# K of 14 head pairs in seven block products, and the exchange ahead of the q load, in a gated cross-attention kernel

## What is computed

```
x = _rmsnorm(hidden_states, ln_weight)
h_q = (x @ w_q.T).reshape(b, lq, H, DH)
h_k = (key_value_states @ w_k.T).reshape(b, lk, H, DH)
h_v = (key_value_states @ w_v.T).reshape(b, lk, H, DH)
score = jnp.einsum('bqhd,bkhd->bhqk', h_q, h_k) + position_bias[None]
score = softmax(where(m, score, -inf))
attn = jnp.einsum('bhqk,bkhd->bqhd', score, h_v).reshape(b, lq, H * DH)
return hidden_states + attn @ w_out.T
```

## Time and profile before

| | |
|---|---|
| median of 3 runs | 897.46 us |
| the profiled execution: its time | 903.37 us |
| its span, first to last instruction | 901.6 us |
| PE busy | 871.0 us (97%) |
| DVE, ACT, POOL busy | 54%, 40%, 33% |
| mean granted clock of PE | 0.998 |

### The profile page before, as it was taken

How to read it: one execution, slowest core, us unless ns; L and a number is a source line. 1 busy time by engine, 2 the same in 40 slices (tenths; PEclk the granted TensorE clock), 3 DMA queues, 4 the chain that set the end, 5 groups by cost and what they waited for, 6 DMA issues and landing times.

```text
span 901.6 us, 15022 instructions
## 1 busy us (share of the span) xinstructions
PE 871.0 (97%) x5128; PEld 769.5 (85%) x5128; DVE 486.7 (54%) x847; ACT 358.9 (40%) x966; POOL 301.2 (33%) x216
## 2 busy tenths in 40 slices
PE   8999999998999999999999999999999999999998
PEld 7878888887888988898989889898889898898786
DVE  6886565573627272636354362726263535577863
ACT  5654444553434342425253343434242525354320
POOL 1476665663232323314132323232231413332200
PEclk9999999999999999999999999999999999999999
DMA  9134545555243333424251524333342425151101
GB/s 312 39 105 158 179 151 175 174 176 198 67 150 99 116 116 99 154 85 146 69 183 37 187 65 151 110 105 122 108 148 76 154 61 190 35 201 34 38 24 70
DMA packets 50673, 109.69 MB, mean 122 GB/s; under 512 B 6752, under 2 KB 24160, under 8 KB 48736
## 3 DMA queue, kind: packets, MB, share of 16 engines
q1 hardware_dynamic: 50656, 109.47, 37.0%
HBM read 75.89 MB, written 33.55 MB: 121 GB/s over the span
## 4 chain that ended last, share of the span: by engine, by line
PE 64%; DMA 14%; DVE 12%; issue 4%; SPq 2%; ACT 1%; POOL 1%; DVEq 0%; POOLq 0%
PE proj_ps L1134 34%; PE proj_ps L1307 15%; DMA block_spill<-block_sb 9%; DMA attn<-block_spill 5%; DVE attn L912 3%; PE score_ps L1193 3%; PE proj_ps L1485 2%; PE turn_ps L1193 2%; PE pv_ps L1193 2%; DVE block_sb L932 2%; SPq L318 2%; DVE attn L926 2%; PE turn_ps L1165 1%; PE proj_ps L1503 1%; DMA acc<-in_x 1%
## 5 line engine op out<-in xcount | busy, mean ns | idle before, releaser
L372 POOL TENSOR_TENSOR w_lo<-w_raw,w_hi 128x1024 fp32r<-128x1024 f32 x49 | 117.1, 2391 | 312.9 <-ACT w_hi L466 312.8
L1134 PE MATMUL proj_ps<-w_hi,ct_hi 128*128 128x256 f32 x512 | 146.4, 286 | 0.0
L1134 PE MATMUL proj_ps<-w_hi,ct_lo 128*128 128x256 f32 x512 | 145.0, 283 | 0.0
L1134 PE MATMUL proj_ps<-w_lo,ct_hi 128*128 128x256 f32 x512 | 145.0, 283 | 0.0
L383 POOL TENSOR_TENSOR comb<-mask_add,bias_sb 128x1024 f32<-128x1024 f32 x32 | 76.7, 2417 | 131.4 <-DVE attn L926 127.6
L486 ACT ACTIVATE attn<-attn,neg_max 128x128 f32<-128x128 f32 x256 | 99.2, 389 | 52.6 <-DVE neg_max L915 52.6
L948 DVE TENSOR_TENSOR acc<-proj_ps,acc 128x512 f32<-128x512 f32 x112 | 77.5, 692 | 66.7 <-PE proj_ps L1134 65.8
L466 ACT ACTIVATE w_hi<-w_raw 128x1024 fp32r<-128x1024 f32 x49 | 51.8, 1059 | 121.9 <-PE proj_ps L1134 118.9
L1134 PEld LDWEIGHTS proj_ps<-w_hi,ct_hi 128*128 128x128 f32 x512 | 98.4, 192 | 0.7
L1134 PEld LDWEIGHTS proj_ps<-w_hi,ct_lo 128*128 128x128 f32 x512 | 98.3, 192 | 0.7
L1134 PEld LDWEIGHTS proj_ps<-w_lo,ct_hi 128*128 128x128 f32 x512 | 98.2, 192 | 0.0
(11 more groups left out here) (204 smaller groups left out, 1781.2 us busy)
## 6 DMA issues: line engine op xcount, KB each, us to landing
w_raw<-in_weights SPq DMA_DIRECT2D x67, 512.0 KB, 3.7
q_spill<-attn SPq DMA_DIRECT2D x60, 256.0 KB, 3.0
qt<-q_spill SPq DMA_DIRECT2D x15, 1024.0 KB, 7.9
block_spill<-block_sb SPq DMA_DIRECT2D x30, 512.0 KB, 4.0
attn<-block_spill SPq DMA_DIRECT2D x120, 128.0 KB, 2.9
acc<-in_x SPq DMA_DIRECT2D x4, 512.0 KB, 9.8
bias_sb<-in_bias SPq DMA_DIRECT2D x16, 128.0 KB, 2.9
out<-attn SPq DMA_DIRECT2D x8, 256.0 KB, 2.0
```

The source lines that it names most:

```text
L372: pool.tensor_tensor(lo, w_raw[:, k, :], hi.bitcast(F32), ALU.subtract).then_inc(w_lo_done[k], 1)
L1134: mm = pe.matmul(o, lhs(l, n), rhs(r, n), start=(start and n == 0 and m == 0), stop=(stop and n == terms - 1 and m == 2))
```

## The change

**K in seven products.** For pairs 2 to 15 (turns p = 2 to 15, index i = p - 2) k is made as q is: `k_stage(p)` makes seven products of 2 blocks x 3 = 6 matmuls, 42 of 512 columns. The products use five banks for results (`proj_ps1` twice, `proj_ps3` twice, `proj_ps2`, and the score banks `turn_ps` and `pv_ps`), so `pv_bank` gives the pv units the other order of banks (score_ps0, score_ps1, turn_ps, pv_ps). Turn 1 keeps the four chunks and is written out on each engine; the loops run from 2.

**Forms of the weights.** POOL makes four sums of 128x256 blocks (`ks_forms`, lines 490 to 495 of the changed file) and seven lo halves of 128x256 (line 500), ACT seven hi halves (line 742), a turn ahead, in place of one 128x1024 of each (`lead(WK)`, `rest(WK)`). ACT further takes three copies in place of four k copies, DVE four sums of products (`k_posts`), POOL one (`k_last_sum`, 128x512).

**Forms of the context.** T1 to T4 are made once, from float32 halves of the context that SP loads again (`load_block` 0 and 1 early in the q loop, 2 ahead of the last `q_phase`, 3 in turn 1): DVE subtracts, ACT leads (`lead_kt`), POOL rests (`rest_kt`), all 128x1024. Form 0 is made in the last `q_phase`, the others in turn 1.

**Order.** In a turn SP does the exchange first and the q load behind it; PE makes two v products ahead of `pv(a, 0)` in place of one. The weights of the last stage (`WQ` of NPH, `WK` of NPH) are split in the last turn; x is reloaded into `mask_add` for two of the eight tiles. In the last turn POOL waits for `probs_done` before `add_mask(LAST)` and adds `k_last_sum` behind it, and PE waits for it (`k_sum`) ahead of `scores(LAST, 0)`.

The diff, cut to its core:

```diff
@@ SP
+            load_block(0, k_buf[:, 0:2, :], 0, 0)
+            load_block(1, k_buf[:, 2:4, :], 0, 1)
...
+            sp.wait_ge(qa_lo, NQ * AF)
+            sp.wait_ge(s_step, NQ * SF)
+            load_block(2, w_raw[:, WQ, :].rearrange("p (c s) -> p c s", c=2), 1, 1)
...
-            with sp.Fori(1, LAST) as p:
-                load_q(p)
+            def turn(p):
                 for t in range(2):
                     exchange(p - 1, t)
+                if isinstance(p, int):
+                    sp.wait_ge(kt_done, 3)
+                    sp.wait_ge(kt_hi_done, 1)
+                    sp.wait_ge(kt_lo_done, 1)
+                    load_block(3, k_buf[:, 0:2, :], 1, 0)
+                load_q(p)
                 load_bias(p + 1)
-                refill(WK, p + 2)
+                sp.wait_ge(k_lo, p * PRODUCTS)
+                load_w(WK, p + 2)
                 refill(WV, p + 2)
                 refill(WO, p + 1)
@@ POOL
+            def k_last_sum(i):
+                pool.wait_ge(k_copied, i * COPIES + 2)
+                pool.wait_ge(k_post, i * KPOSTS + 2)
+                pool.tensor_tensor(kt[:, 1, half(1)], k_w, k_v, ALU.add).then_inc(k_sum, 1)
+
+            rest_kt(0, 1)
             pool.wait_ge(mask_done, 1)
             add_mask(0)
             rest(WK, 1)
             rest(WV, 1)
             rest(WO, 0)
...
+            with pool.Fori(2, LAST) as p:
                 pool.wait_ge(probs_done, (p - 1) * UNITS + UNITS)
                 add_mask(p)
-                for k in (WK, WV):
-                    rest(k, p + 1)
+                k_last_sum(p - 2)
+                k_forms(p - 1)
+                rest(WV, p + 1)
                 rest(WO, p)
@@ ACT, iteration(p)
                 exps(a, 0)
                 exps(a, 1)
+                k_copy(i, 1, s_copy, k1_ps)
                 exps(a, 2)
-                chunk(0)
+                k_copy(i, 2, k_w, k5_ps)
                 exps(a, 3)
-                chunk(1)
-                chunk(2)
-                chunk(3)
-                lead(WK, p + 1)
+                k_copy(i, 6, k_at(0), k1_ps)
                 lead_at(a, 0)
                 lead_at(a, 1)
...
+                v_copy(p, 1)
+                lead_k(i + 1)
                 lead_at(a, 2)
                 lead_at(a, 3)
@@ DVE, behind turn_probs(a, 1)
+            def k_posts(i):
...
+                post(4, k_t, k6_ps, s_copy)
+                post(5, k_v, k7_ps, k_t)
+                post(3, kt[:, 1, half(0)], k4_ps, k_v)
+                post(7, kt[:, 0, half(1)], k5_ps, k_t)
@@ PE
+            def k_product(o, w, x, start=True):
+                for c in range(2):
+                    for m, (l, r) in enumerate(((0, 0), (1, 0), (0, 1))):
+                        mm = pe.matmul(o[:, :], w[l][:, c, :], x[r][:, c, :], start=(start and c == 0 and m == 0),
+                                       stop=(c == 1 and m == 2), skip_group_check=not start)
+                mm.then_inc(k_prod, 1)
...
+                k_product(k1_ps, KA11, KB11)
+                k_product(k5_ps, KS1, KT1)
+                k_product(k4_ps, KA22, KT4)
+                k_product(k6_ps, KS2, KT2)
+                k_product(k7_ps, KS3, KT3)
+                k_product(k1_ps, KA12, KB21, False)
+                k_product(k5_ps, KS4, KB22, False)
...
-                chunk(UNITS)
-                pv(a, 0)
-                pv(a, 1)
-                chunk(UNITS + 1)
-                chunk(UNITS + 2)
-                chunk(UNITS + 3)
+                v_chunk(p, 0)
+                v_chunk(p, 1)
+                pv(a, 0)
+                pv(a, 1)
+                v_chunk(p, 2)
+                v_chunk(p, 3)
                 pv(a, 2)
                 pv(a, 3)
```

More of the change, by code:

```diff
@@ L195, in build @@
         q_prod, q_copied, q_post, q_in = sem("q_prod"), sem("q_copied"), sem("q_post"), sem("q_in")
+        kc_in = [sem(f"kc_in{n}") for n in range(4)]
+        kt_done, kt_hi_done, kt_lo_done = sem("kt_done"), sem("kt_hi_done"), sem("kt_lo_done")
+        ks_step, k_hi, k_lo = sem("ks_step"), sem("k_hi"), sem("k_lo")
+        k_prod, k_copied, k_post, k_sum = sem("k_prod"), sem("k_copied"), sem("k_post"), sem("k_sum")
         q_stored = {k: sem(f"q_stored{k[0]}{k[1]}") for k in ((0, 0), (0, 1), (1, 0), (1, 1))}
@@ L575, in _, with lead_kt @@
             lead_s(0, 2)
+            def lead_kt(n, place):
+                act.wait_ge(kt_done, place)
+                act.activation(kt_form_at(0, n), kt_raw[n], ACT.Copy).then_inc(kt_hi_done, 1)
             def product(i, n):
@@ new lines, in v_copy, with first_turn, k_chunk @@
+            def v_copy(p, m):
+                copy_proj(p, m, m, v_dst(m))
+            def first_turn():
+                def k_chunk(u):
+                    act.wait_ge(proj_done, PROJ0 + (u + 1))
+                    act.activation(k_at(u), proj_ps[u][:, :], ACT.Copy).then_inc(proj_copied, 1)
+                exps(0, 0)
+                exps(0, 1)
+                exps(0, 2)
+                k_chunk(0)
+                exps(0, 3)
+                for u in range(1, UNITS):
+                    k_chunk(u)
+                lead_kt(2, 2)
+                lead_kt(1, 3)
+                lead_at(0, 0)
+                lead_at(0, 1)
+                v_copy(1, 0)
+                v_copy(1, 1)
+                lead_at(0, 2)
+                lead_at(0, 3)
+                lead_kt(3, 4)
+                v_copy(1, 2)
+                v_copy(1, 3)
+                lead(WV, 2)
+                lead_k(0)
+                act.wait_ge(out_done, B)
+                lead(WO, 1)
@@ L676, in _ @@
             exps(LAST, 1)
+            for k in (WK, WQ):
+                act.wait_ge(w_in[k], 16 * (NPH + 1))
+                act.activation(w_hi[:, k, :], w_raw[:, k, :], ACT.Copy).then_inc(w_hi_done[k], 1)
             lead_at(LAST - 1, 2)
@@ new lines, in _, with bank_added @@
+            KA11, KA12, KA22 = (tuple(columns(w, WK, n) for w in (w_hi, w_lo)) for n in range(AF))
+            KS1, KS2, KS3, KS4 = (tuple(columns(w, WQ, n) for w in (w_hi, w_lo)) for n in range(SF))
+            KB11, KB21, KB22 = (tuple(x[:, 2 * k:2 * k + 2, half(t)] for x in ct2) for k, t in ((0, 0), (1, 0), (1, 1)))
+            KT1, KT2, KT3, KT4 = (tuple(kt_form_at(s, n) for s in range(2)) for n in range(TF))
+            def bank_added(p, b):
+                pe.wait_ge(acc_done, (p - 1) * B + (B - BANKS + b + 1))
@@ new lines, in v_chunk @@
+            def v_chunk(p, m):
+                if isinstance(p, int) and p == 1:
+                    pe.wait_ge(proj_copied, PROJ0 + (m + 1))
+                elif m == 0:
+                    bank_added(p, 0)
+                elif m == 1:
+                    pe.wait_ge(k_copied, (p - 2) * COPIES + COPIES)
+                else:
+                    pe.wait_ge(k_post, (p - 2) * KPOSTS + (m + 1))
+                if m == 0:
+                    pe.wait_ge(w_lo_done[WV], p + 1)
+                v_pair(m, m)
```

257 lines of the change are left out of this document (189 added, 68 removed).

## The result

| | before | after |
|---|---|---|
| median | 897.48 us (897.05 to 898.23) | 865.10 us (863.80 to 865.76) |
| the profiled execution: its time | 903.37 us | 864.54 us |
| its span | 901.6 us | 862.8 us |
| mean granted clock of PE | 0.998 | 1.000 |

Four runs each. The ratio is 0.9637, 95% interval 0.962 to 0.9653: the kernel is 3.6% faster, and the forecast of 865.6 us lies half a microsecond off.

A forecast was written before the change was run, and what follows sets the result against it. PE was taken to bound the kernel, a turn being 40.7 us of matmuls and 1.1 of waiting. The terms -19.1 - 14.0 - 0.1 + 1.2 + 0.1 = -31.9 took the median 897.46 to 865.6 us, range 861.5 to 872.

The forecast's parts named there:

- Matmuls, -19.1: K in turns 2 to 15: 48 matmuls become 42, 14 x 6 x 0.228 us, saving 19.1 us.
- The PV wait, -14.0: PE's wait for the probabilities, 1.08 us in each of 13 turns, goes, with two microseconds in hand: -14.0 us.
- I take the 5.9 between them as unchanged: The profiled run's 903.37 us stood 5.9 above the median of 897.46; the sum carried that excess over unchanged.
- the 39.3 to 39.5: Sign that the forecast is right: steady turns of 39.3 to 39.5 us.
- Turn 1, -0.1: Turn 1: old wait and slower PE gone (-4.4, -1.6), new stalls +2.7, +0.5, +0.8, +1.9; -0.1 us, bounds -4 and +5.
- the terms taken as half likely: In turn 1: 0.5 us of wait at PV (from 0 to 1.5) and 0.8 of lower clock (from 0 to 1.6).
- Turn 2, +1.2: Turn 2: late POOL halves and weight loads delay the exchange's start and write, against 2.4 in hand; +1.2 us, bounds 0 and 4.
- The last turn, +0.1: Last turn: `k_sum` comes at +18.6, PE at +18.8; cost +0.1 us, bounds 0 and 1.5.
- The opening, 0: Early context loads in the q loop and new code at the second loop's start: cost 0, bounds -0.5 and +1.5.
- The dear opening: Rival: stalls of turns 1 and 2 at their upper bounds, priced at 6 us more, 871.6 us; chance 15%.
- The lock: Rival: DVE operations with two SBUF inputs and POOL exclude each other, the PV wait stays; 879.6 us; chance 9%.
- The late forms: Rival: ACT's seven K forms wait for slow POOL sums, delaying the third v copy in each turn; 947 us; chance 3%.

The follow-up runs named there:

- experiment 1: The kernel before with one edit: in the loop turns SP does the exchange ahead of the q load; 882.47 us, ratio 0.985.
- experiment 2: The kernel before with one edit: two v products ahead of PV in the loop turns, q load still ahead of the exchange; 880.44 us, ratio 0.9813.
- experiment 5: The kernel before, unchanged, profiled a second time; 897.15 us, a span of 895.3.
- experiment 4: The changed kernel with only the q load moved back ahead of the exchange; 869.52 us, ratio 0.9689.
- experiment 6: The changed kernel with only the second v product moved back behind PV, so one stands ahead of it; 869.47 us, ratio 0.967.
- run 10: The changed kernel with eight unused 128x512 additions on POOL ahead of the K sums in each loop turn; 937.63 us, ratio 1.0438.
- run 3: The changed kernel with the q load ahead of the exchange and one v product ahead of PV, in every turn but the last; 908.15 us, ratio 1.0135.
- run 7: The changed kernel with context form 0's POOL half moved behind turn 1's lo halves and ACT's fourth-form lead behind its last two V copies; 861.33 us, ratio 0.9577.
- run 8: The changed kernel with four unused 128x512 additions on POOL ahead of the K sums in each loop turn; 866.24 us, ratio 0.9636.
- run 9: The kernel before with both order edits (exchange ahead of the q load, two v products ahead of PV), without the changed K products; 879.10 us, ratio 0.9791.
- run 11: The changed kernel with only ACT's lead of the fourth context form moved behind its last two V copies in turn 1; 864.18 us, ratio 0.9628.

## Why the prediction was right

Faster was forecast at 0.96, 865.6 us in a range of 861.5 to 872.0; it is 865.10. Point by point:

- **Matmuls, -19.1: right.** 9.54 us in place of 10.93 in each turn, 1.36 apart between kernels with no wait (40.47 and 39.11). The Trainium skill's figure (TensorE: Matmul & The Clock Gate, back-to-back matmuls), 215.7 ns, would give 1.29; the trace decides for 0.228 a matmul.
- **The PV wait, -14.0: the place right, the size right for this profile and too large for the median.** All of the wait went, and experiments 1 and 2 show that either edit is enough in the steady turns, which the margin of 2 us in the text had implied. The step that was off is the write of the first half: I took 3.6 us from the second half, and it took 2.6. The 3.6 was not a write by itself. In the earlier trace rows the second write goes out 1.9 us behind the first of the reads, while these are still landing; in the steady turns of the changed kernel it goes out 2.8 us behind and takes 2.7 (485.52 to 488.20). The q load does not make the difference: in turn 2 of the changed kernel it stands behind both halves, the second write is again 1.9 us behind the first read, and takes 3.55. The kernel before, then turn 2 of the changed kernel:

```profile
504.44 1.75 SPq L318 DMA_DIRECT2D attn<-block_spill  x4
```

```profile
250.72 1.75 SPq L343 DMA_DIRECT2D attn<-block_spill  x4
252.58 0.36 SPq L339 DMA_DIRECT2D block_spill<-block_sb  x1
256.13 1.73 SPq L343 DMA_DIRECT2D attn<-block_spill  x4
```

- **One turn for all, in the same term:** the landing was read from a single turn's rows, where the write varied by 1.4 us from turn to turn. PE comes to `pv` at +18.86 (predicted +18.8).
- **"I take the 5.9 between them as unchanged": wrong.** They were in the wait (experiment 5) and went with it, so that the profiled executions are 38.8 us apart and the medians 32.4.
- **Missing term: the restart behind the wait.** `pv` ran 0.26 us faster in each steady turn, 3.4 in all, and so the steady turn of 39.11 lies below the 39.3 to 39.5 that was to show the forecast right. It stood in the earlier trace rows (1.16 for the first eight matmuls, 2.06 for the sixteen), and turn 1's own 1.6 was counted, but not these.
- **Turn 1, -0.1: -1.5 measured.** Each stage was right within a microsecond. The sum is off by the terms taken as half likely: no clock loss, no wait at `pv`, 1.4 in place of 1.9. DVE's 2.85 us operation beside POOL came as drawn (200.34, the normalising). The second of the two starts at 203.51, behind the end of POOL's halves (202.65), and takes 0.69.
- **Turn 2, +1.2: 0 measured.** 39.11 us. What was feared came, at two thirds: the first write goes out 0.75 us late (+9.31) and takes 4.52 in place of 2.62, 2.65 in all. The turn's cover, 2.4 by the forecast, was in truth near 3.3 (landing at +15.6, PE at +18.86) and took it. Experiments 4 and 6 show that it was needed: with either edit undone turn 2 loses 1.6 or 2.2 us.
- **The last turn, +0.1: right.** -1.2 measured, of which -1.37 are the products, which the sum had under matmuls. **The opening, 0:** -1.0 measured, not explained; the executions differ by such amounts ahead of turn 1 (first scores from 191.3 to 192.9 in runs whose code up to there is that of the changed kernel, 191.6 to 192.8 with that of the kernel before).
- **Net, against the execution of before that lies near the median** (experiment 5, 895.3 to 862.8, -32.5): turns 2 to 14 give 13 x -2.29 = -29.8 (1.36 products, about 0.68 wait, 0.25 restart), where the sum had 13 x -2.45 = -31.8. Turn 1 gives -0.7 (-0.1), turn 2's cost is 0 (+1.2), the opening -0.8 (0), the last turn and tail -1.2 (-1.3). Errors of 2.1 one way and 2.6 the other: the mechanism was right, that the time is right to half a microsecond is luck.
- **The rivals.** The dear opening didn't come, though experiments 4 and 6, each without one edit, land two microseconds short of its 871.6. The lock shows in turn 1 (DVE operations of 2.47 us at 193.24 and 2.85 at 200.34, beside POOL's) and by 0.7 us in turn 2, and never in turns 3 to 14. The late forms are shown by run 10, as an edit of ours and not of the change. What the text didn't have is the worse of the partial changes: K alone, with the wait left in, is 1.3% slower than before.

## What to carry to other kernels

Work taken away ahead of a wait buys nothing until the wait is gone, and here it bought less than nothing, because the longer waits brought the lower clock behind some of them. So remove the wait first, then the work. When two edits each remove a wait wholly, credit it once, and look for what the second one covers: here it was the first turns, in which other engines are late. And before carrying a profile's excess over the median into a sum as unchanged, see in which wait it lies.

## What the runs showed of the hardware

- **A 512 KB write from the same queue as a 1 MB read:** 3.4 to 6.0 us, another value in each turn, when issued 3.6 us behind the read (kernel before, runs 2 and 5; in runs 3 and 4, at 3.7 us behind, from 2.8 and 3.3 up), and 2.62 to 2.64 in each of the turns 3 to 14 with the read behind it; the read itself 7.9 and 5.2 us by the medians. Other traffic counts as well: the same write took 4.5 us right behind three weight loads (turn 2 of the changed kernel), and 3.55 at 1.9 us behind the first of four 128 KB reads where it took 2.7 at 2.8 us behind.
- **What stands behind a wait of PE** in these traces, for 16 matmuls of 128 columns: 1.79 us without one, 2.06 behind a wait of 1.1. On top of this comes, at times, a stretch at the lower clock (granted clocks of 0.72 to 0.92 in windows of 6 to 20 us). Behind the waits of 1.9 to 2.6 us at `pv` and at the start of k it came in 8 of 18, an equal wait of 2.6 us bringing it in one execution and not in another; it came behind each wait of 3.4 us and more, and behind none of 1.8 or less. It cost 1.3 to 2.6 us each time, which belongs in the price of such a wait.
- **Scatter of the turns follows the wait.** PE's wait in the kernel before copied the write's scatter, with turns from 40.6 to 42.3 us. The changed kernel and the runs 1, 2, 6, 7, 8, 9 and 11, with no wait in turns 3 to 14, have these turns equal to 0.01 us (run 4, at its tie, to 0.2). For whole executions the case shows less: within 1.2 us of one another in run 9, which has no such wait at all, but 4.4 apart in run 1 and 5.7 (895.9 to 901.7) in the kernel before over the jobs.
